# The first loads and the first steps of a cross-attention kernel in another order

## What is computed

```python
q = (layernorm(x) @ Wq).reshape(B, N, 16, 64)
k = (context @ Wk).reshape(B, M, 16, 64)
v = (context @ Wv).reshape(B, M, 16, 64)
sim = einsum('bihd,bjhd->bhij', q, k) * 64 ** -0.5
x = x + einsum('bhij,bjhd->bihd', softmax(sim), v).reshape(B, N, 1024) @ Wo
```

## Time and profile before

| | us |
|---|---|
| median of 3 runs | 447.81 (447.59 to 449.85) |
| the profiled execution | 448.28 |
| span of its instructions | 446.5 |
| TensorE busy | 428.5 (96%) |
| VectorE busy | 338.2 (76%) |
| ACT busy | 246.2 (55%) |
| GpSimd busy | 138.5 (31%) |

### The profile page before, as it was taken

The page is one execution under the profiler, slowest core; times in us unless marked ns, Lnnn a source line. Parts: engine busy times, 40 slices in busy tenths (PEclk is TensorE's granted clock), DMA queues, the critical chain, the costliest instruction groups (busy, mean ns, idle before and its releaser), DMA issues.

```text
span 446.5 us, 7523 instructions
## 1 busy us (share of the span) xinstructions
PE 428.5 (96%) x3038; PEld 391.6 (88%) x3038; DVE 338.2 (76%) x618; ACT 246.2 (55%) x421; POOL 138.5 (31%) x76
## 2 busy tenths in 40 slices
PE   2899999999999999999999999999999999899997
PEld 2788899999999999889999998989999888798986
DVE  2567777786786767767898688988997999668871
ACT  2366555665565456645664665636755654633641
POOL 2509000503050005030704053255340343446740
PEclk9999999999999999999999999999999999999999
DMA  8162200111011001110110011000100001476000
GB/s 215 62 157 22 71 19 12 21 63 18 13 16 67 19 12 20 64 18 13 13 70 19 12 13 69 19 1 15 13 18 3 10 13 31 82 196 182 1 3 21
DMA packets 15110, 19.05 MB, mean 43 GB/s; under 512 B 3954, under 2 KB 10882, under 8 KB 15076
## 3 DMA queue, kind: packets, MB, share of 16 engines
q1 hardware_dynamic: 14788, 17.53, 16.1%
q10 hardware_dynamic: 288, 1.05, 0.8%
HBM read 18.32 MB, written 0.26 MB: 42 GB/s over the span
## 4 chain that ended last, share of the span: by engine, by line
PE 78%; DVE 10%; ACT 5%; DMA 2%; issue 2%; POOL 2%; POOLq 1%; ACTq 0%
PE turned L626 15%; PE scores L614 8%; PE acc L648 8%; PE acc L647 8%; PE acc L646 8%; PE scores L616 8%; PE scores L615 8%; PE misc L663 3%; PE misc L551 3%; DVE small L1226 2%; PE misc L688 2%; DVE pT_l L1236 2%; PE misc L545 2%; ACT prob L1002 2%; DMA wk_sb<-in_L_xattn_Wk_dram 2%
## 5 line engine op out<-in xcount | busy, mean ns | idle before, releaser
L995 ACT CAST pT_h<-turned 125x512 fp32r<-125x512 f32 x168 | 94.9, 589 | 122.5 <-PE turned L626 121.8
L1236 DVE TENSOR_TENSOR pT_l<-turned,pT_h 125x512 fp32r<-125x512 f32 x168 | 112.2, 687 | 59.5 <-ACT pT_h L995 59.0
L1226 DVE TENSOR_REDUCE small<-scores 128x1 f32<-128x500 f32 x168 | 109.2, 674 | 11.2 <-PE scores L616 11.0
L626 PE MATMUL turned<-ident,prob 128*125 128x128 f32 x672 | 94.7, 276 | 2.9 <-DVE pT_l L1236 2.6
L626 PEld LDWEIGHTS turned<-ident,prob 128*125 128x125 f32 x672 | 87.4, 187 | 10.6 <-DVE pT_l L1236 4.3
L646 PE MATMUL acc<-pT_h,ctx_nh 125*128 125x256 f32 (+1 forms) x288 | 94.6, 329 | 0.0
L1002 ACT ACTIVATE prob<-scores,small 128x1500 f32<-128x1500 f32 x56 | 84.9, 1516 | 13.4 <-DVE small L1229 13.4
L648 PE MATMUL acc<-pT_h,ctx_nl 125*128 125x256 f32 (+1 forms) x288 | 86.5, 300 | 0.0
L647 PE MATMUL acc<-pT_l,ctx_nh 125*128 125x256 f32 (+1 forms) x288 | 86.3, 300 | 0.0
L614 PE MATMUL scores<-ctx_th,qk_h 128*128 128x500 f32 x168 | 68.2, 406 | 1.9 <-DVE qk_l L1219 1.2
L616 PE MATMUL scores<-ctx_th,qk_l 128*128 128x500 f32 x168 | 65.3, 389 | 0.0
(11 more groups left out here) (164 smaller groups left out, 536.8 us busy)
## 6 DMA issues: line engine op xcount, KB each, us to landing
ctx_raw<-in_ctx_dram SPq DMA_DIRECT2D x7, 750.0 KB
rbc<-rden_row SPq DMA_DIRECT2D x15, 128.0 KB, 3.2
rbc<-rden_row SPq DMA_DIRECT2D x8, 192.0 KB, 3.2
eb<-in_L_ffn_expert_b_dram SPq DMA_DIRECT2D x4, 256.0 KB, 5.8
ctx_raw<-in_ctx_dram SPq DMA_DIRECT2D x3, 250.0 KB
wq_sb<-in_L_xattn_Wq_dram ACTq DMA_DIRECT2D x1, 512.0 KB, 4.8
wk_sb<-in_L_xattn_Wk_dram ACTq DMA_DIRECT2D x1, 512.0 KB, 8.7
wv_sb<-in_L_xattn_Wv_dram SPq DMA_DIRECT2D x1, 512.0 KB, 9.4
```

What stands on the lines that cost most here:

```text
L626: last = tr(turned[0:CK, m, 128 * c:128 * c + 128], prob[u][:, CK * j:CK * j + CK], ident[:, :])
L995: nc.scalar.copy(pT_h[0:CK, PLACES[g // NT % 2][t], CPB * k:CPB * k + CPB, :], turned[0:CK, (KB * u + k) % 2, :].rearrange("p (c r) -> p c ...
L1226: m = v.tensor_reduce(bankmax[:, u, k:k + 1], scores[:, k, 0:KW], AX.X, ALU.max)
L1236: v.tensor_tensor(pT_l[0:CK, place, dst, :], turned[0:CK, (KB * u + k) % 2, :].rearrange("p (c r) -> p c r", c=CPB), pT_h[0:CK, place, dst ...
```

## The change

SP waits for Wq to have landed before it issues the first ctx piece, and so Wv and Wo. In the head TensorE turns x and makes the first head products before it turns the first two pieces of ctx, and ACT and VectorE copy and split in that order. The scores of tile 0 wait for ctx piece by piece instead of for all three. ACT copies the second eight heads' wqk behind the exp of tile 0 instead of before it. The turning of Wv goes from steps 0 and 1 to step 1, a `make_qk` each from steps 0 and 1 to steps 1 and 2, the first turning of the second batch's ctx from step 2 to 3, the second from step 3 to 4, and the copies with them. The second half of Wv and the last head products go by other banks (M1, M0).

```diff
--- before.py
+++ after.py
@@ -337,6 +337,7 @@
         @block.sync
         def _(sp):
             sp.dma_start(x_sb[:, :, :], x_v).then_inc(x_in, 16)
+            sp.wait_ge(wq_in, 16)
             for k in range(KB):
                 chunks = slice(CPB * k, CPB * k + CPB)
                 sp.dma_start(ctx_raw[:, chunks, :], ctx_v[0][:, chunks, :]).then_inc(ctx0_in[k], 16)
@@ -587,14 +588,15 @@
             pe.wait_ge(wk_in, 16)
             turn_weight(wk_sb, 0, S2)
             turn_weight(wk_sb, 1, T0)
-            turn_ctx(0, 0, 1, first=True)
             pe.wait_ge(xn_ready, 1)
             for q in range(NQ):
                 last = tr(bank(ACC)[:, PT * q:PT * q + PT], xn[:, q, :], ident[0:PT, 0:PT])
             last.then_inc(setup_pe, 1)
+            pe.wait_ge(setup_act, 3)
+            pe.wait_ge(setup_dve, 1)
+            head_pairs(wqT, wkT, 0, T1, S0)
+            turn_ctx(0, 0, 1, first=True)
             turn_ctx(0, 1, 0, first=True)
-            pe.wait_ge(setup_act, 3)
-            head_pairs(wqT, wkT, 0, T1, S0)
             pe.wait_ge(ctxT_lo, 1)
             turn_ctx(0, 2, 1, first=True)
             pe.wait_ge(setup_act, 4)
@@ -611,6 +613,8 @@
                 for k in range(KB):
                     o = scores[:, k, 0:KW]
                     keys = slice(KW * k, KW * k + KW)
+                    if g == 0:
+                        pe.wait_ge(ctxT_lo, k + 1)
                     mm(o, hi, ctx_th[a][:, keys], start=True, stop=False)
                     mm(o, hi, ctx_tl[a][:, keys], start=False, stop=False)
                     mm(o, lo, ctx_th[a][:, keys], start=False, stop=True).then_inc(scores_pe, 1)
@@ -784,49 +788,50 @@
                     u = (g + 1) % 2
 
                     if t == 0:
-                        pe.wait_ge(ctxT_lo, KB * (b + 1))
+                        if b > 0:
+                            pe.wait_ge(ctxT_lo, KB * (b + 1))
                         if a == 1:
                             pe.wait_ge(qkb_lo, i + 1)
                     if a == 0:
                         pe.wait_ge(qk_lo, i * 4 + rounds_of_qk(t))
                     make_scores(g, a, t)
 
+                    if g == 1:
+                        pe.wait_ge(setup_act, 5)
+                        pe.wait_ge(setup_dve, 4)
                     if before:
                         turn_probs(g - 1, u, 0)
                         turn_probs(g - 1, u, 1)
                     mid_step(b, t)
                     if first:
                         if t == 0:
+                            pe.wait_ge(ctxT_lo, KB)
                             make_qk(0, 1, 1)
-                            pe.wait_ge(setup_dve, 1)
                             head_pairs(wqT, wkT, 2, T0, T1)
+                        if t == 1:
                             pe.wait_ge(wvo_in, 32)
                             turn_weight(wv_sb, 0, ACC)
-                            pe.wait_ge(setup_act, 5)
-                            pe.wait_ge(setup_dve, 4)
-                            pe.wait_ge(qk_lo, 1)
+                            pe.wait_ge(qk_lo, 2)
+                            turn_weight(wv_sb, 1, M1)
                             make_qk(0, 2, 0)
-                        if t == 1:
+                        if t == 2:
                             pe.wait_ge(setup_act, 6)
-                            turn_weight(wv_sb, 1, ACC)
-                            pe.wait_ge(qk_lo, 2)
-                            make_qk(0, 3, 1)
-                        if t == 2:
                             pe.wait_ge(setup_dve, 5)
                             head_products(wvT, wo_sb, 0, ACC)
+                            make_qk(0, 3, 1)
                             pe.wait_ge(qk_lo, 3)
                             head_products(wvT, wo_sb, 2, M0)
-                            pe.wait_ge(qk_lo, 4)
-                            turn_ctx(1, 0, 1)
                         if t == 3:
                             pe.wait_ge(setup_act, 7)
                             head_products(wvT, wo_sb, 1, ACC)
+                            pe.wait_ge(qk_lo, 4)
+                            turn_ctx(1, 0, 1)
                             pe.wait_ge(setup_dve, 6)
+                            head_products(wvT, wo_sb, 3, M0)
+                        if t == 4:
+                            pe.wait_ge(setup_dve, 7)
                             turn_ctx(1, 1, 0)
                             pe.wait_ge(ctxT_lo, KB + 1)
-                            head_products(wvT, wo_sb, 3, M1)
-                        if t == 4:
-                            pe.wait_ge(setup_dve, 7)
                             turn_ctx(1, 2, 1)
                             pe.wait_ge(setup_act, 8)
                     part = share(b, t)
@@ -1102,17 +1107,18 @@
                         hi_probs(g - 1, 1 - u, (t - 1) % NT, 2)
                     if first:
                         if t == 0:
+                            copy_out(8, wqk[:, 8:16:2, :], T0, SCALE)
+                        if t == 1:
                             copy_out(10, wvT[:, 0:4, :], ACC)
                             hi_qk(0, 2, 0)
-                        if t == 1:
-                            hi_qk(0, 3, 1)
                         if t == 2:
                             copy_out(12, wvo[:, 0:8:2, :], ACC)
-                            hi_ctx(1, 1, 0, 1)
+                            hi_qk(0, 3, 1)
                         if t == 3:
                             copy_out(14, wvo[:, 1:8:2, :], ACC)
+                            hi_ctx(1, 1, 0, 1)
+                        if t == 4:
                             hi_ctx(1, 1, 1, 0)
-                        if t == 4:
                             hi_ctx(1, 1, 2, 1)
                     else:
                         end_step(b, t)
@@ -1120,13 +1126,12 @@
             copy_out(1, wqT[:, 0:4, :], S0)
             copy_out(2, wqT[:, 4:8, :], S1)
             copy_out(3, wkT[:, 0:4, :], S2)
+            copy_out(6, wqk[:, 0:8:2, :], T1, SCALE)
             hi_ctx(0, 0, 0, 1)
             hi_ctx(0, 0, 1, 0)
-            copy_out(6, wqk[:, 0:8:2, :], T1, SCALE)
             hi_ctx(0, 0, 2, 1)
             hi_qk(0, 0, 0)
             hi_qk(0, 1, 1)
-            copy_out(8, wqk[:, 8:16:2, :], T0, SCALE)
             for b in range(B):
                 half(b, first=(b == 0))
             G = B * NT
@@ -1402,25 +1407,25 @@
                         if t == 0:
                             lo_qk(0, 1, 1)
                             copy_out(9, wqk[:, 9:16:2, :], T1, SCALE)
+                        if t == 1:
+                            copy_out(11, wvT[:, 4:8, :], M1)
                             lo_qk(0, 2, 0)
-                        if t == 1:
-                            copy_out(11, wvT[:, 4:8, :], ACC)
+                        if t == 2:
                             lo_qk(0, 3, 1)
-                        if t == 2:
                             copy_out(13, wvo[:, 8:16:2, :], M0)
+                        if t == 3:
                             lo_ctx(1, 1, 0, 1)
-                        if t == 3:
+                            copy_out(15, wvo[:, 9:16:2, :], M0)
+                        if t == 4:
                             lo_ctx(1, 1, 1, 0)
-                            copy_out(15, wvo[:, 9:16:2, :], M1)
-                        if t == 4:
                             lo_ctx(1, 1, 2, 1)
 
             copy_out(4, wkT[:, 4:8, :], T0)
-            lo_ctx(0, 0, 0, 1)
             dve.wait_ge(setup_pe, 5)
             v.tensor_copy(xnT[:, :], bank(ACC)[:, 0:TOK]).then_inc(setup_dve, 1)
+            copy_out(7, wqk[:, 1:8:2, :], S0, SCALE)
+            lo_ctx(0, 0, 0, 1)
             lo_ctx(0, 0, 1, 0)
-            copy_out(7, wqk[:, 1:8:2, :], S0, SCALE)
             lo_ctx(0, 0, 2, 1)
             lo_qk(0, 0, 0)
             for b in range(B):
```

## The result

| | before | changed |
|---|---|---|
| median, 20 runs each | 447.88 us (447.02 to 449.85) | 450.39 us (447.94 to 452.48) |
| ratio | | 1.0045, 95% interval 1.0031 to 1.0058 |
| profiled execution | 448.28 us, span 446.5 | 448.12 us, span 446.3 |

What follows compares the result with a forecast made beforehand. TensorE was taken to bound the kernel from 25.15 us on, order of events before 18.64. Terms -1.2 - 0.9 + 0.44 + 0.44 + 0.26 + 0.7 = -0.26 us gave a 447.6 us median, range 446.0 to 450.2.

Steps and rivals of the forecast that it cites:

- The likeliest case: Whole kernel: the forecast of 447.6 us, together with its neighbour of ctx landing as now (448.1); chance 0.70.
- the second rival, the clock: First q-k product and nine score matmuls: TensorE back at 1.2 GHz after waits, +3.0 us, 450.5 in all; chance 0.10.
- Wk, x, Wq: Opening loads, issued alone: Wk lands at 7.2 us instead of 9.9, Wq at 5.1, x at 5.4.
- ctx at 14.6: Head: ctx, sharing memory with Wv and Wo, lands at 14.6 us, bounds 12.9 and 18.1; third ctx turn starts then.
- the head: Start to first scores: third ctx turn and first q-k product come earlier, first scores near 17.4 us; -1.2 us.
- ctx late, the bound: Head, a rival: held-back ctx lands at 18.1 us, head +2.5 instead of -1.2, 451.3 in all; chance 0.08.
- The head products: Head: products follow the x turns and take 1.14 us, from 10.1 to 11.3 us, ahead of the ctx turns.
- Step 0: First to second scores: tile 0's exp no longer waits behind the wqk copy and sets the step, 5.6 us; -0.9 us.
- Step 1: Second to third scores, TensorE full: one more group of Wv turns; +0.44 us.
- Step 2: Third to fourth scores: TensorE swaps a ctx turn for a q-k product; +0.44 us.
- Step 4: Fifth to sixth scores: TensorE turns two ctx pieces instead of one, with 0.18 us idle; +0.26 us.
- Step 5: Sixth to seventh scores, on VectorE: two low parts of ctx ahead of the row maxima; +0.7 us, bounds 0 and 0.7.

Runs made afterwards that it cites:

- again: The changed kernel once more, unedited, to profile a slower execution: 450.85 us, ratio 1.0066 to the kernel before.
- wv_in_step0: Kernel before's head and SP order with the changed steps, but both Wv turns in step 0: 447.67 us, ratio 1.0001.
- head_alone: Kernel before with SP's wait and the changed head, its steps as before: 450.25 us, ratio 1.0056.
- steps_refilled: Kernel before with tile 0's exp ahead of the wqk copy, both Wv turns in step 0, both remaining q-k rounds in step 1: 447.42 us, ratio 0.9986.
- filled: Changed kernel with TensorE's idle time filled by Wq turns nobody reads, in the head and step 0: 448.08 us, ratio 1.0014 to the kernel before.
- wait_alone: Kernel before with SP's wait for Wq and nothing else of the change: 449.57 us, ratio 1.0035.
- fill_more: The filled kernel with more idle Wq turns ahead of the second and third ctx turns: 449.20 us, ratio 1.0022 to the kernel before.
- no_wait: Changed kernel without SP's wait for Wq: 449.24 us, ratio 1.0024 to the kernel before.

## Why the prediction was wrong

The likeliest case failed; the second rival, the clock, is what happened, and it had a chance of 0.10. Two of the prediction's own signs of being wrong are in the traces: the third ctx turn after 15.5 (15.68 in the quick profile) and the nine first score matmuls near 4 us long instead of 2.1 (19.05 to 22.97 in again).

- **Wk, x, Wq.** Wk at 7.2: its turns began at 7.39, not waiting. x and Wq I had guessed earlier; xn turns began at 9.83 for 9.2.
- **ctx at 14.6.** It landed at 15.68, inside the bounds (12.9 to 18.1), 1.1 us late. This is the mis-sized term of the sum: the head gave 0.35 us and not 1.2. The issue was 0.24 us later than assumed (5.54 for 5.3); the rest is the transfer, for which 17.6 KB/us for each engine was too high (about 16 by the same working, an estimate). That about five engines carry ctx fits the tail at a third of 16 engines, and cutting the rows removed the tail.
- **ctx late, the bound.** The +2.5 for a landing at 18.1 is a slip: 18.1 + 0.55 + 2.31 - 18.64 is +2.3, and that rival's time 451.1 instead of 451.3. It changes nothing here.
- **The head products.** I used the 1.14 us of the earlier trace rows; in the quick profile they took 2.0 (10.77 to 12.78), the engine not yet having risen. It cost nothing, since ctx came later still.
- **Step 0** -0.9: -1.05. **Step 1** +0.44: +0.13. **Step 2** +0.44: +0.50. **Step 4** +0.26: 0.00. **Step 5** +0.7: +0.59. I called step 1 full of TensorE work; wv_in_step0 shows that its 4.97 us are bound by the exp as well. First scores by pieces were worth nothing as far as the profile tells: the scores waited for q-k.
- **The sum** of -0.26 against -0.16 in an execution at 1.000: two errors of opposite sign, the head 0.85 too good and the steps 0.74 too dear, so the close agreement is luck. Against the medians, the executions at 1.000 are 0.3 us above the kernel before and not 0.26 below.
- **The step that failed is the weighing of the clock.** I saw the sparse stretch from 11.3 to 17.4 and priced its fall at 3.0 us (450.5; the median is 450.39, the groups are 1.4, 2.5 and 4.3 us above the first), but put it at 0.10 since 1.2 us of idle time between the product and the scores had done no harm before. That compared a single gap with a row of gaps: TensorE is busy for 1.81 of the 5 us from 11 to 16 in the slow profile, and its longest wait alone is 2.05. I also counted the busy run ahead of the gaps as protection; in again the rise came in that run already, TensorE finished the head sooner and had longer to wait. And I read one profile with a clock of 1.00 as what the kernel does, where a program can have a place at which each execution falls or does not.

The price of one fall was right: in again the first scores come 0.76 us later than in the quick profile and the second 2.67 us later, for the 3.0 priced. That the median hits 450.5 so closely is partly luck, since it depends on how many executions fall and in which way. The range ended at 450.2, and the median lies 0.19 us above it.

## What to carry to other kernels

When a change makes TensorE's beginning sparser, count the idle microseconds of the whole stretch, not the longest gap alone, take a sparse stretch as a risk and not as a verdict (head_alone's profile fell with less idle time than the quick one), and ask for the granted clock of many executions; one profile can be the lucky one. The best filling of an idle stretch is needed work, because it also shortens what comes later (1.2 us from tile 0 to tile 7 in steps_refilled); idle work only guards the clock, and is free only where nothing needed is queued behind it. Here a load of 125 rows kept about a third of the DMA engines busy (a share of 0.33 from 14 to 16 us); cut into 112 and 13 rows, all of ctx was there at 11.48 instead of 15.71.

## What the runs showed of the hardware

- The clock falls in or right behind a sparse stretch, not only when TensorE is busy again: in again it is 1.00 with 0.23 us of work in the two from 14 and 0.57 in the three from 16, with TensorE back at 15.77; in filled it is already 0.56 from 15 to 16, with 0.05 us of work.
- The mean granted clock of an execution does not hold a stretch before the first rise: wait_alone's profile says 1.000 with four ctx turns in 1.09 us at 16.88, where they take 0.65 at full clock. The execution of 835.26 us has rows at 1.00 and matmuls at about half speed for most of its length. Durations decide.
- The moment of the first rise differs between executions of one kernel: the x turns take 0.62 us at 9.50 in again and 1.01 at 9.83 in the quick profile, where the head products still take 0.42 each until 12.4. The early rise came with the longer time in that pair. With fills the same early rise kept its clock through the head (fill_more's profile).
- Not settled: why all 7 executions of no_wait and all 12 of wv_in_step0 were at 1.000, but 6 of 12 of steps_refilled at 0.996, and where the 7 of 106 of the kernel before at 0.996 fall. Only one profile of steps_refilled shows the place, near 386 us.
